# Layernorm finish and upsampling blend moved to VectorE, and a denser timetable, in a fused multi-scale attention kernel

## The chip, the core and the metric

The kernel runs on one core of a Trainium2 chip. TensorE (PE) multiplies, VectorE (DVE), ScalarE (ACT) and GpSimd (POOL) work on vectors, SyncE (SP) issues the DMAs. The metric is the time of one launch on the device in microseconds, the median of several runs.

## The reference

Eight sequences of 1024 tokens with 256 features go through a four-level attention, a residual layernorm, a feed-forward network and another residual layernorm. The part that the change touches is this:

```python
outs = []
for lvl in range(4):                        # strides 1, 2, 4, 8
    x = query[:, ::2**lvl, :]               # 1024, 512, 256, 128 tokens
    outs.append(_mha(x, in_w[lvl], in_b[lvl], out_w[lvl], out_b[lvl]))   # 16 heads of 16
current = outs[-1]
for lvl in (2, 1, 0):
    current = _upsample_linear(current, outs[lvl].shape[1])   # 0.75 near + 0.25 far
    current = current @ up_w[lvl].T + up_b[lvl]
    current = current + outs[lvl]
x = _layernorm(query + current)             # (x - mean) / sqrt(var + 1e-5), no gain
# then the gated feed-forward network and a second layernorm
```

## The kernel before, in words

The attention part lasts to about 2850 us of the span, the feed-forward part from there to the end; the change lies in the attention part alone. It works on one batch element after the other. The attention of one element is cut into 85 steps: a unit is a group of four heads and (at level 0) one half of 1024 query tokens, and a step is one block of 128 keys of a unit. In each step PE computes four 96x512 blocks of scores for the row maxima (L1015), four of the scores themselves (L1000), and eight value products (L1032); ACT takes two exponentials of 128x1024 (L760); DVE takes the four maxima over 512 columns (L839). The maxima's PSUM tile `p_m` has two halves: PE writes one while DVE reads the other.

Everything else is spread over the steps as side work. The projections (`proj`), value tiles (`v`), negated maxima (`neg`), output matmuls per level (`mid`), upsampled parts (`lift`, `row`) and the last output (`out`) each take one PSUM tile `p_a` in a step of its own. After each unit DVE transposes and normalizes its result (`turn`, `invert`, `spread`), POOL multiplies it (`attn`, L657).

The loop over the batch elements is software-pipelined: a prefix, a loop of seven bodies, and an end. A body runs from step 26.9 of one element to step 26.9 of the next, so the output part of an element runs at steps 10 to 24 of the next. Inside a body the order of the instructions is written by `timeline()`: it gives each task a time in steps, `places()` moves side jobs to free steps, and each engine sorts its tasks by that time plus an offset out of the table `LATER`. Each engine then does its tasks strictly in this order, waiting on semaphores for what the others have to deliver.

The output part of an element, in four jobs of 256 tokens, passes through these tasks: `fetch` (SP, six DMAs: the input tokens and the upsampled rows in two parts, L594 to L598), `sum` (POOL, two additions, L700 and L703, into a ring `s_ring` of four slots of 128 tokens; in the trace it is part of `a_c_f`), `out` (PE matmul, then DVE's addition, L879, which waits for `xt_summed`), and per half `stats` (DVE bn_stats L882, later POOL's power for rstd, L706, and the shift, L710), `gather` (DVE bn_aggr and the variance plus eps, L888 and L890), `finish` (ACT's scale and shift in place, L803, then SP's store to x1, L602). The sum of job n+2 waits for the stores of job n, as it writes over the same ring slots (`y_stored`). The half jobs are numbered 0 to 7.

`blend` builds the upsampled tokens of levels 3 and 2: ACT writes a part scaled by 0.75 and one scaled by 0.25 with scaled biases, and POOL adds shifted pieces of them (four additions for level 3, six for level 2). `scale` (two ACT operations of 128x1024, L808 and L810) and `keep` (SP) write the level 1 rows to memory, scaled by 0.75 and 0.25, from where `fetch` reads them.

## Time and profile before

| | us |
|---|---|
| median of three runs (4295.5 to 4300.24) | 4297.32 |
| the profiled execution | 4300.24 |
| its span | 4298.4 |
| PE busy | 3855.2 (90%) |
| DVE busy | 2566.8 (60%) |
| ACT busy | 2483.7 (58%) |
| POOL busy | 1211.1 (28%) |
| mean granted TensorE clock | 0.955 |

The profiled execution is one launch. Its span goes from its first to its last instruction, and what lies around it makes up the rest of its time. Times in the trace count from the span's start. Engines work beside each other, so the busy times do not add up. In a timeline row the bracket says how long the engine was idle ahead of the instruction and what released it; x2 is two instructions of the same kind in a row, and their time is given together.

### The profile page before, as it was taken

Reading aid. Unit: us, or ns where it says so; the run is one execution under the profiler, and the core shown is the slowest. Engines: PE = TensorE matmul, PEld = TensorE weight load, DVE = VectorE, ACT = ScalarE, POOL = GpSimd, SP = SyncE. Lnnn points to the kernel's source line nnn. Section 1 sums busy time; section 2 is a strip of 40 time slices with the busy share of each in tenths; the row PEclk is TensorE's granted clock in tenths of the full one; section 3 lists DMA queues with packets and bytes.
Section 4 is the critical chain, followed back from the end, with each engine's and each line's share of the span. In section 5 each row is a group of like instructions: output and inputs, shape, how many; then the busy total and the mean of one; then the engine's idle time right before and its main releaser. Section 6 shows DMA issues by size and latency. Waiting matters only on the chain. (4 is left out here: it accounts for less than half of the span.)

```text
span 4298.4 us, 69980 instructions
## 1 busy us (share of the span) xinstructions
PE 3855.2 (90%) x20881; PEld 2139.9 (50%) x20881; DVE 2566.8 (60%) x4681; ACT 2483.7 (58%) x3261; POOL 1211.1 (28%) x1144
## 2 busy tenths in 40 slices
PE   4589999989989999999999999918999999999998
PEld 2233334334333433333333333206887877877887
DVE  2377787787787787787787788643333333333333
ACT  1367767767767767767767766724444443444443
POOL 4234434435435434434434442210000000000000
PEclk6699999999999999999999999958999999999999
DMA  5344343344334344344344343151000000000000
GB/s 172 105 82 104 94 93 91 101 89 95 106 74 108 97 85 97 103 87 92 108 91 87 108 88 62 38 200 43 11 21 11 11 11 21 11 11 11 14 17 11
DMA packets 308845, 307.48 MB, mean 72 GB/s; under 512 B 75169, under 2 KB 285281, under 8 KB 308193
## 3 DMA queue, kind: packets, MB, share of 16 engines
q1 hardware_dynamic: 299200, 293.59, 27.7%
q10 hardware_dynamic: 9216, 8.39, 0.6%
q8 instruction: 243, 3.98, 0.4%
q14 instruction: 186, 1.52, 0.1%
HBM read 202.28 MB, written 96.47 MB: 70 GB/s over the span
## 5 line engine op out<-in xcount | busy, mean ns | idle before, releaser
L760 ACT ACTIVATE a_probs<-a_p_s 128x1024 f32<-128x1024 f32 x1360 | 1322.4, 1020 | 610.4 <-PE a_p_s L1000 603.2
L839 DVE TENSOR_REDUCE a_part_max<-a_p_m 128x1 f32<-128x512 f32 x2048 | 1338.5, 680 | 434.6 <-PE a_p_m L1015 429.7
L1015 PE MATMUL a_p_m<-a_k_st,a_q_st 96*128 96x512 bf16 (+2 forms) x2944 | 1010.3, 375 | 184.5 <-DVE a_part_max L839 85.4
L1395 PE MATMUL p_h<-f_h_hi,f_w_hi 128*128 128x512 f32 x2048 | 809.9, 395 | 40.0 <-issue 35.2
L1000 PE MATMUL a_p_s<-a_q_st,a_k_st 98*128 98x512 bf16 (+2 forms) x2944 | 822.2, 367 | 11.0 <-DMA a_q_st<-a_neg_bf 6.8
L1395 PE MATMUL p_h<-f_h_lo,f_w_hi 128*128 128x512 f32 x2048 | 806.3, 394 | 1.6 <-issue 1.6
L1015 PEld LDWEIGHTS a_p_m<-a_k_st,a_q_st 96*128 96x128 bf16 x2944 | 258.7, 97 | 1085.2 <-DVE a_part_max L839 692.0
L1032 PE MATMUL a_p_o<-a_probs,a_v_aug 128*17 128x512 f32 (+2 forms) x5888 | 729.3, 575 | 0.8 <-ACT a_probs L760 0.8
L1364 DVE TENSOR_TENSOR f_h_lo<-f_h_f,f_h_hi 128x512 fp32r<-128x512 f32 x256 | 177.1, 692 | 720.3 <-ACT f_h_hi L1277 720.3
L839 DVE TENSOR_REDUCE a_row_max<-a_p_m 128x1 f32<-128x512 f32 (+2 forms) x672 | 439.9, 680 | 176.3 <-PE a_p_m L1015 171.6
L1275 ACT ACTIVATE f_h_f<-p_h,f_sc 128x512 f32<-128x512 f32 x256 | 176.6, 690 | 583.2 <-PE p_h L1395 583.1
L1395 PEld LDWEIGHTS p_h<-f_h_hi,f_w_hi 128*128 128x128 f32 x2048 | 390.0, 190 | 110.5 <-issue 29.3
L1395 PEld LDWEIGHTS p_h<-f_h_lo,f_w_hi 128*128 128x128 f32 x2048 | 390.2, 191 | 97.3 <-issue 16.6
L1216 POOL TENSOR_TENSOR f_rstd<-f_var_eps,f_minus_half 128x1 f32<-128x1 f32 x64 | 35.1, 549 | 1410.3 <-DVE f_var_eps L1355 1410.3
L1000 PEld LDWEIGHTS a_p_s<-a_q_st,a_k_st 98*128 98x128 bf16 x2944 | 282.6, 99 | 264.6 <-ACT a_probs L760 25.5
L653 POOL TENSOR_TENSOR a_neg_bf<-a_neg_f,a_neg_bf 4x512 bf16<-4x512 f32 x120 | 138.0, 1150 | 365.7 <-ACT a_neg_bf L755 365.1
L643 POOL TENSOR_TENSOR a_qk<-a_qk,a_qk_bf 128x512 f32<-128x512 f32 x120 | 139.1, 1159 | 332.9 <-ACT a_qk_bf L748 332.9
L1032 PEld LDWEIGHTS a_p_o<-a_probs,a_v_aug 128*17 128x17 f32 x5888 | 103.2, 96 | 221.9 <-ACT a_probs L760 132.5
L908 PE MATMUL a_p_a<-a_x_hi,a_w_hi 128*128 128x512 f32 (+2 forms) x320 | 139.7, 437 | 78.2 <-POOL a_w_lo L632 61.2
L1395 PE MATMUL p_h<-f_xt_hi,f_w_hi 128*128 128x512 f32 x512 | 200.9, 392 | 1.4 <-DVE f_xt_lo L1316 1.4
L1395 PE MATMUL p_h<-f_xt_lo,f_w_hi 128*128 128x512 f32 x512 | 200.6, 392 | 0.0
L657 POOL TENSOR_TENSOR a_attn<-a_raw,a_attn 128x512 f32<-128x512 f32 x120 | 152.8, 1273 | 146.6 <-DVE a_attn L868 146.6
(116 smaller groups left out, 4552.5 us busy)
## 6 DMA issues: line engine op xcount, KB each, us to landing
qk_scratch<-a_qk_bf SPq DMA_DIRECT2D x96, 384.0 KB, 2.8
a_w_lo<-wqkv_inner SPq DMA_DIRECT2D x32, 768.0 KB, 4.3
a_q_st<-qk_scratch SPq DMA_DIRECT2D x192, 128.0 KB, 6.1
a_k_st<-qk_scratch SPq DMA_DIRECT2D x192, 128.0 KB, 6.5
a_q_st<-qk_scratch SPq DMA_DIRECT2D x336, 64.0 KB, 2.6
a_k_st<-qk_scratch SPq DMA_DIRECT2D x336, 64.0 KB, 2.7
a_a_lo<-a_attn SPq DMA_DIRECT2D x384, 32.0 KB, 1.9
a_o_lo<-wo_inner SPq DMA_DIRECT2D x24, 512.0 KB, 3.5
```

Of the source, the lines that this page charges most:

```text
L643: pool.tensor_tensor(out=rest, in0=rest, in1=bf[:, 0, :], op=ALU.subtract)\
L653: pool.tensor_tensor(out=neg_bf[:, n % 2, 1, :], in0=neg_f[:, :], in1=neg_bf[:, n % 2, 0, :], op=ALU.subtract).then_inc(neg_b.sem, 1)
L657: pool.tensor_tensor(out=attn[:, n % RING, :], in0=raw[:, n % 2, :], in1=attn[:, n % RING, :], op=ALU.mult)\
L760: act.activation(probs[:, s % 2, 2 * p:2 * p + 2, :], p_s[:, 2 * p:2 * p + 2, :], ACT.Exp, scale=HD ** -0.5).then_inc(exp_done.sem, 1)
L839: dve.reduce_max(out, src, AX.X).then_inc(max_read.sem, 1)
L908: ins = pe.matmul(out, a, c, start=n == 0, stop=n == len(terms) - 1)
L1000: ins = pe.matmul(p_s[:, j, i * size:(i + 1) * size], k_st[0:ROWS + 2, unit.halves[half], j, key:key + 128], q_st[0:ROWS + 2, unit.place, ...
L1015: ins = pe.matmul(p_m[:, n % 2, r * size:(r + 1) * size], q_st[0:ROWS, unit.place, j, q * 128:(q + 1) * 128], k_st[0:ROWS, unit.halves[kb] ...
L1032: ins = pe.matmul(p_o[32 * j:32 * j + HD + 1, at], v_aug[:, V_TILE[lvl] + kt, unit.head + j * parts + i, :], probs[:, n % 2, j, at], start ...
L1275: act.activation(h_f[:, v % 2, :], p_h[:, v % 4, :], ACT.Gelu, scale=sc[:, 8 + v:9 + v]).then_inc(deep_read.sem, 1)
L1364: dve.tensor_tensor(out=h_lo[:, (half + v // 8) % 2, v % 8, :], in0=h_f[:, v % 2, :], in1=h_hi[:, (half + v // 8) % 2, v % 8, :], op=ALU.s ...
L1395: ins = pe.matmul(out, a, c, start=first and n == 0, stop=last and n == len(terms) - 1)
```

## The change

The timetable changes in these places: the offset of POOL's `attn` (0.8) goes; the output jobs want places 3 steps apart, not 4 (they land at steps 10, 13, 16 and 19, before at 10, 14, 18 and 22, and two value jobs, `v`, go from 15 and 19 to 14 and 18); `row` 0 and 1 go from steps 66 and 67 to 64 and 66, `proj` 7 from 68 to 67, and `scale` and `keep` one step earlier. `finish` comes 1.8 steps behind its output job rather than 2.9. `fetch` 1 is later (step 90.65, not 83.3), `fetch` 3 and the sums are earlier. The tasks of `blend` follow each other at .15 steps, not .8.

Three tasks change engine or form. `blend` goes from POOL to DVE: ACT writes the upsampled part once, with the plain bias; DVE scales a copy by 0.75 and adds shifted pieces with a multiplication by 0.25 in the same instruction (scalar_tensor_tensor). `finish` goes from ACT to DVE, as a tensor_scalar that subtracts the mean and multiplies by rstd; so POOL's shift goes, and so does DVE's wait for a finished half ahead of `gather`. The last maximum of a level 0 unit, a reduction of 128x32 to 128x16, is a tensor_tensor with the operation max of the two columns.

```diff
@@ -214,7 +214,7 @@
 LATER = {
     "act": {"proj": .3, "neg": .2, "mid": .3, "lift": .3, "acut": .5},
     "dve": {"v": .3, "row": .3, "out": .3},
-    "pool": {"proj": .9, "neg": .6, "mid": .9, "ccut": .5, "acut": .8, "attn": .8, "xcut": .4, "wcut": .4, "ocut": .4, "stats": 1},
+    "pool": {"proj": .9, "neg": .6, "mid": .9, "ccut": .5, "acut": .8, "xcut": .4, "wcut": .4, "ocut": .4, "stats": 1},
...
@@ -240,14 +240,14 @@
     out_at = STEPS + 10
-    side.update(places([(("out", n), out_at + 4 * n) for n in range(4)], taken))
+    side.update(places([(("out", n), out_at + 3 * n) for n in range(4)], taken))
...
-            side.update(places([(("row", n), mid_at[lvl] + 6 + 2 * n) for n in range(2)], taken))
+            side.update(places([(("row", n), mid_at[lvl] + 5 + 2 * n) for n in range(2)], taken))
...
@@ -289,15 +289,15 @@
-            p += [(side[("lift", i)] + 1.5 + .8 * n, "blend", n + RUNS_DONE[lvl] - len(RUNS[lvl])) for n in range(len(RUNS[lvl]))]
+            p += [(side[("lift", i)] + 1 + .15 * n, "blend", n + RUNS_DONE[lvl] - len(RUNS[lvl])) for n in range(len(RUNS[lvl]))]
...
         at = side[("out", n)]
-        sum_at = 83 if n == 0 else at - 2.1
-        p.append((78 if n == 0 else (83 if n == 1 else side[("out", n - 1)] - 2.1) + .3, "fetch", n))
+        p.append((78 if n == 0 else max(sum_at, side[("out", n - 1)] - 6) + .8, "fetch", n))
+        sum_at = 83 if n == 0 else at - 1.5
         p.append((sum_at, "sum", n))
         for half in range(2):
-            p += [(at + .4 + .7 * half, "stats", 2 * n + half), (at + .75 + .7 * half, "gather", 2 * n + half), (at + 2.9 + .5 * half, "finish", 2 * n + half)]
+            p += [(at + .4 + .7 * half, "stats", 2 * n + half), (at + .75 + .7 * half, "gather", 2 * n + half), (at + 1.8 + .5 * half, "finish", 2 * n + half)]
...
-                        elif kind == "blend":
-                            lvl = 3 if n < RUNS_DONE[3] else 2
-                            run = n - (0 if lvl == 3 else RUNS_DONE[3])
-                            if run == 0:
-                                lift_read.wait(pool, it, 1 if lvl == 3 else 2)
...
-                            pool.tensor_tensor(out=fine[lvl - 1][:, :, dst:dst + size], in0=d_f[:, :, src:src + size],
-                                               in1=d_part[:, :, here:here + size], op=ALU.add).then_inc(fine_done.sem, 1)
...
-                            pool.wait_ge(rstd_done.sem, rstd_done.value(it, n + 1))
-                            pool.sem_inc(held.sem, 1)
-                            pool.tensor_scalar(shift[:, n % 2:n % 2 + 1], moments[:, n % 2, 0:1], rstd[:, n % 2:n % 2 + 1], -1.0, ALU.mult, ALU.mult)\
-                                .then_inc(shift_done.sem, 1)
...
-                                act.activation(d_part[:, m, 0:S], p_a[:, m * S:(m + 1) * S], ACT.Identity, bias=col_near[:, lvl - 1, m:m + 1], scale=0.75)
-                                ins = act.activation(d_f[:, m, 0:S], p_a[:, m * S:(m + 1) * S], ACT.Identity, bias=col_far[:, lvl - 1, m:m + 1], scale=0.25)
+                                ins = act.activation(d_f[:, m, 0:S], p_a[:, m * S:(m + 1) * S], ACT.Identity, bias=col[:, lvl - 1, CUP + m:CUP + m + 1])
                             ins.then_inc(lift_read.sem, 1)
-                        elif kind == "finish":
-                            act.wait_ge(shift_done.sem, shift_done.value(it, n + 1))
-                            act.activation(s_ring[:, n % 4, :], s_ring[:, n % 4, :], ACT.Identity, bias=shift[:, n % 2:n % 2 + 1],
-                                           scale=rstd[:, n % 2:n % 2 + 1]).then_inc(y_done.sem, 1)
...
-                                dve.reduce_max(slot, part_max[:, u % RING, :, :], AX.X).then_inc(max_done.sem, 1)
+                                dve.tensor_tensor(out=slot, in0=part_max[:, u % RING, :, 0], in1=part_max[:, u % RING, :, 1], op=ALU.max)\
+                                   .then_inc(max_done.sem, 1)
...
-                            y_done.wait(dve, it, n - 1)
-                            dve.sem_inc(held.sem, 1)
...
+                        elif kind == "finish":
+
+                            dve.wait_ge(rstd_done.sem, rstd_done.value(it, n + 1))
+                            dve.tensor_scalar(s_ring[:, n % 4, :], s_ring[:, n % 4, :], moments[:, n % 2, 0:1],
+                                              rstd[:, n % 2:n % 2 + 1], ALU.subtract, ALU.mult).then_inc(y_done.sem, 1)
+                        elif kind == "blend":
+                            lvl = 3 if n < RUNS_DONE[3] else 2
+                            run = n - (0 if lvl == 3 else RUNS_DONE[3])
+                            S = tokens(lvl)
+                            if run == 0:
+                                lift_read.wait(dve, it, 1 if lvl == 3 else 2)
+                                dve.tensor_scalar(d_part[:, :, 0:S], d_f[:, :, 0:S], 0.75, None, ALU.mult).then_inc(part_done.sem, 1)
+
+                                if lvl == 3:
+                                    xt_summed.wait(dve, earlier(it), 4)
+                                else:
+                                    kept.wait(dve, earlier(it), 1)
+                                part_done.wait(dve, it, 1 if lvl == 3 else 2)
+                            src, dst, size, here = RUNS[lvl][run]
+                            dve.scalar_tensor_tensor(out=fine[lvl - 1][:, :, dst:dst + size], in0=d_f[:, :, src:src + size],
+                                                     scalar=0.25, in1=d_part[:, :, here:here + size],
+                                                     op0=ALU.mult, op1=ALU.add).then_inc(fine_done.sem, 1)
```

What the order is around finish 3 on DVE (step 16). The value job is L849 before and L821 after, the maxima L839 and L810. Before:

```order
L849 TENSOR_TENSOR a_v_aug<-a_p_a,a_row 128x16x16 [waits a_value_mm]
L849 TENSOR_TENSOR a_v_aug<-a_p_a,a_row 128x16x16
L186 REGISTER_ALU
L888 BN_AGGR a_moments<-a_stats 128x2 [waits a_y_done,a_stats_done]
L890 TENSOR_SCALAR a_var_eps<-a_moments 128x1 [waits a_moments_done]
L829 REGISTER_ALU
L839 TENSOR_REDUCE a_part_max<-a_p_m 128x1 [waits a_max_mm]
L829 REGISTER_ALU
L839 TENSOR_REDUCE a_part_max<-a_p_m 128x1 [waits a_max_mm]
L842 TENSOR_REDUCE a_row_max<-a_part_max 128x16 [waits a_max_read]
```

After, where L865 is the finish (the first is finish 2, the second finish 3):

```order
L860 TENSOR_SCALAR a_var_eps<-a_moments 128x1 [waits a_moments_done]
L800 REGISTER_ALU
L810 TENSOR_REDUCE a_part_max<-a_p_m 128x1 [waits a_max_mm]
L800 REGISTER_ALU
L810 TENSOR_REDUCE a_part_max<-a_p_m 128x1 [waits a_max_mm]
L865 TENSOR_SCALAR a_c_f<-a_c_f,a_moments,a_rstd 128x256 [waits a_rstd_done]
L800 REGISTER_ALU
L810 TENSOR_REDUCE a_part_max<-a_p_m 128x1 [waits a_max_mm]
L800 REGISTER_ALU
L810 TENSOR_REDUCE a_part_max<-a_p_m 128x1 [waits a_max_mm]
L865 TENSOR_SCALAR a_c_f<-a_c_f,a_moments,a_rstd 128x256 [waits a_rstd_done]
L800 REGISTER_ALU
```

Two finishes that wait for rstd stand among the maxima; before, there is none on this engine.

POOL, from the attention product ahead of sum 2. L706 is rstd, L710 shift, L700 and L703 are the sum. Before:

```order
L657 TENSOR_TENSOR a_attn<-a_raw,a_attn 128x512 [waits a_spread_done]
L705 REGISTER_ALU
L706 TENSOR_TENSOR a_rstd<-a_var_eps,a_minus_half 128x1 [waits a_eps_done]
L710 TENSOR_SCALAR a_shift<-a_moments,a_rstd 128x1 [waits a_rstd_done]
L696 REGISTER_ALU
L186 REGISTER_ALU [waits a_fetched]
L700 TENSOR_TENSOR a_c_f<-a_d_room 128x512 [waits a_y_stored0,a_y_stored1]
L703 TENSOR_TENSOR a_c_f<-a_c_f,a_fine_room 128x512 [waits a_half_sum]
L705 REGISTER_ALU
L706 TENSOR_TENSOR a_rstd<-a_var_eps,a_minus_half 128x1 [waits a_eps_done]
L710 TENSOR_SCALAR a_shift<-a_moments,a_rstd 128x1 [waits a_rstd_done]
```

After, with L690 as rstd and L684 and L687 as the sum; the first L690 is rstd 2, the one behind sum 2 is rstd 3, then rstd 4:

```order
L655 TENSOR_TENSOR a_attn<-a_raw,a_attn 128x512 [waits a_spread_done]
L689 REGISTER_ALU
L690 TENSOR_TENSOR a_rstd<-a_var_eps,a_minus_half 128x1 [waits a_eps_done]
L680 REGISTER_ALU
L186 REGISTER_ALU [waits a_fetched]
L684 TENSOR_TENSOR a_c_f<-a_d_room 128x512 [waits a_y_stored0,a_y_stored1]
L687 TENSOR_TENSOR a_c_f<-a_c_f,a_fine_room 128x512 [waits a_half_sum]
L689 REGISTER_ALU
L690 TENSOR_TENSOR a_rstd<-a_var_eps,a_minus_half 128x1 [waits a_eps_done]
L689 REGISTER_ALU
L690 TENSOR_TENSOR a_rstd<-a_var_eps,a_minus_half 128x1 [waits a_eps_done]
```

Rstd 3 stands behind sum 2 in both orders. Further down, after only, sum 3 and rstd 5:

```order
L684 TENSOR_TENSOR a_c_f<-a_d_room 128x512 [waits a_y_stored3,a_fetched,a_y_stored2]
L687 TENSOR_TENSOR a_c_f<-a_c_f,a_fine_room 128x512 [waits a_half_sum]
L651 TENSOR_TENSOR a_neg_bf<-a_neg_f,a_neg_bf 4x512 [waits a_neg_hi]
L654 REGISTER_ALU
L655 TENSOR_TENSOR a_attn<-a_raw,a_attn 128x512 [waits a_spread_done]
L689 REGISTER_ALU
L690 TENSOR_TENSOR a_rstd<-a_var_eps,a_minus_half 128x1 [waits a_eps_done]
```

Rstd 5 stands behind sum 3, a negated maximum (L651) and an attention product (L655).

SP, around the loads of stack 8 (twelve DMAs, of which the first and last rows stand). L602 is the store of a finished half. Before:

```order
L598 DMA a_fine_room<-up_far 64x256 x4
L186 REGISTER_ALU [waits a_stored0,a_stored1]
L542 DMA a_q_st<-qk_scratch 16x8x512 [waits a_score_mm]
L542 DMA a_k_st<-qk_scratch 16x8x512
...
L542 DMA a_q_st<-qk_scratch 16x8x512
L542 DMA a_k_st<-qk_scratch 16x8x512
L600 REGISTER_ALU
L602 DMA x<-a_c_f 128x256 [waits a_y_done]
L600 REGISTER_ALU
L602 ISA [waits a_y_done]
L602 DMA x<-a_c_f 128x256
```

After, where L600 is the store and L540 the loads:

```order
L596 DMA a_fine_room<-up_far 64x256 x4
L598 REGISTER_ALU
L600 DMA x<-a_c_f 128x256 [waits a_y_done]
L186 REGISTER_ALU [waits a_stored0,a_stored1]
L540 DMA a_q_st<-qk_scratch 16x8x512 [waits a_score_mm]
L540 DMA a_k_st<-qk_scratch 16x8x512
...
L540 DMA a_q_st<-qk_scratch 16x8x512
L540 DMA a_k_st<-qk_scratch 16x8x512
L598 REGISTER_ALU
L600 ISA [waits a_y_done]
L600 DMA x<-a_c_f 128x256
```

One of the two stores now stands ahead of the twelve loads, the other behind them as before.

## Rows read from the trace of the kernel before

**Rows 1.** The page, part 1: busy time, share and instructions of each engine.

```profile
PE 3855.2 (90%) x20881; PEld 2139.9 (50%) x20881; DVE 2566.8 (60%) x4681; ACT 2483.7 (58%) x3261; POOL 1211.1 (28%) x1144
```

**Rows 2.** Busy times in windows: start:end, length, busy of each, PEclk, DMA share, GB/s.

```profile
1675.00:2000.00 325.00, 304.56 (x1844) 126.73 (x1842) 250.45 (x462) 230.26 (x292) 141.45 (x132) 0.98 0.42 97
```

**Rows 3.** Timeline of ScalarE, 1728 to 1735: start us, duration, line, operation, [idle before <-releaser].

```profile
1728.01 1.94 ACT L760 ACTIVATE a_probs<-a_p_s 128x1024 f32<-128x1024 f32 x2 [0.60 <-PE a_p_s L1000]
...
1731.42 1.94 ACT L760 ACTIVATE a_probs<-a_p_s 128x1024 f32<-128x1024 f32 x2
...
1734.55 1.94 ACT L760 ACTIVATE a_probs<-a_p_s 128x1024 f32<-128x1024 f32 x2 [1.19 <-PE a_p_s L1000]
```

**Rows 4.** Timeline of ScalarE, 1773 to 1797.

```profile
1773.07 1.94 ACT L760 ACTIVATE a_probs<-a_p_s 128x1024 f32<-128x1024 f32 x2 [2.31 <-PE a_p_s L1000]
...
1777.32 1.94 ACT L760 ACTIVATE a_probs<-a_p_s 128x1024 f32<-128x1024 f32 x2 [2.31 <-PE a_p_s L1000]
...
1779.15 1.06 ACT L808 ACTIVATE a_d_room<-a_c_f 128x1024 f32<-128x1024 f32 x1
...
1785.83 0.69 ACT L743 ACTIVATE a_qk<-a_p_a,a_col 128x512 f32<-128x512 f32 x1 [1.53 <-POOL a_qk_bf L649]
...
1797.14 1.94 ACT L760 ACTIVATE a_probs<-a_p_s 128x1024 f32<-128x1024 f32 x2
```

**Rows 5.** Timeline of ScalarE, 1909 to 1944.

```profile
1909.50 1.94 ACT L760 ACTIVATE a_probs<-a_p_s 128x1024 f32<-128x1024 f32 x2
...
1915.50 0.60 ACT L803 ACTIVATE a_c_f<-a_c_f,a_shift,a_rstd 128x256 f32<-128x256 f32 x1 [2.45 <-POOL a_shift L710]
...
1922.33 1.94 ACT L760 ACTIVATE a_probs<-a_p_s 128x1024 f32<-128x1024 f32 x2 [2.06 <-PE a_p_s L1000]
...
1944.02 1.94 ACT L760 ACTIVATE a_probs<-a_p_s 128x1024 f32<-128x1024 f32 x2 [1.19 <-PE a_p_s L1000]
```

**Rows 6.** Busy times in two windows around the slow matmuls of step 23.

```profile
1932.00:1937.00 5.00, 3.17 (x16) 0.82 (x16) 4.93 (x14) 2.71 (x3) 1.80 (x2) 1.00 0.08 20
1937.00:1941.00 4.00, 3.92 (x14) 0.89 (x15) 2.81 (x8) 0.12 (x1) 2.34 (x5) 0.57 0.44 143
```

**Rows 7.** Timeline of SP's queue, 1896 to 1920: DMA issues.

```profile
1896.36 0.64 SPq L542 DMA_DIRECT2D a_q_st<-qk_scratch  x1
...
1904.35 1.07 SPq L602 DMA_DIRECT2D x<-a_c_f  x2
...
1919.58 0.38 SPq L602 DMA_DIRECT2D x<-a_c_f  x1
```

**Rows 8.** The stores of L602, issued 1900 to 1930: from issue to landing.

```profile
DMA to landing us min/median/max: 1.7/5.7/6.9
```

**Rows 9.** Timeline of POOL, 1911 to 1926.

```profile
1911.75 1.26 POOL L700 TENSOR_TENSOR a_c_f<-a_d_room 128x512 f32<-128x512 f32 x1 [7.87 <-DMA x<-a_c_f]
...
1914.44 0.55 POOL L706 TENSOR_TENSOR a_rstd<-a_var_eps,a_minus_half 128x1 f32<-128x1 f32 x1
...
1915.42 1.15 POOL L653 TENSOR_TENSOR a_neg_bf<-a_neg_f,a_neg_bf 4x512 bf16<-4x512 f32 x1
...
1919.77 1.27 POOL L657 TENSOR_TENSOR a_attn<-a_raw,a_attn 128x512 f32<-128x512 f32 x1
...
1926.12 1.26 POOL L700 TENSOR_TENSOR a_c_f<-a_d_room 128x512 f32<-128x512 f32 x1 [4.09 <-DMA x<-a_c_f]
```

**Rows 10.** Waits of POOL, 700 to 2650: total us, times, longest.

```profile
POOL a_c_f L700 <- DMA x<-a_c_f: 72.0, 12, 8.5
```

**Rows 11.** Timeline of VectorE, step 16.

```profile
1905.99 1.29 DVE L839 TENSOR_REDUCE a_part_max<-a_p_m 128x1 f32<-128x512 f32 x2
```

**Rows 12.** VectorE's groups by line, shapes apart: busy us, mean ns of one, idle.

```profile
L1332 DVE SCALAR_TENSOR_TENSOR f_h_f<-p_h,f_sc,f_gate 128x512 f32<-128x512 f32 x128 | 96.1, 751 | 159.6 <-PE p_h L1395 139.8 <-ACT f_gate L1249 19.8
...
L1341 DVE TENSOR_SCALAR f_s_ring<-f_s_ring,f_moments,f_rstd 128x256 f32<-128x256 f32 x64 | 26.1, 408 | 2.7 <-POOL f_rstd L1216 2.7
...
L842 DVE TENSOR_REDUCE a_row_max<-a_part_max 128x16 f32<-128x32 f32 x64 | 11.9, 186 | 2.2
```

More of the change, by code:

```diff
@@ L375, in attention @@
         stats, moments = sb("stats", [128, 2, 6]), sb("moments", [128, 2, 2])
-        var_eps, rstd, shift, minus_half = sb("var_eps", [128, 2]), sb("rstd", [128, 2]), sb("shift", [128, 2]), sb("minus_half", [128, 1])
-        col_near, col_far = sb("col_near", [128, LEVELS, 2]), sb("col_far", [128, LEVELS, 2])
+        var_eps, rstd, minus_half = sb("var_eps", [128, 2]), sb("rstd", [128, 2]), sb("minus_half", [128, 1])
         d_f, d_part = d_room[:, 0:512].rearrange("p (c t) -> p c t", c=2), d_room[:, 512:1024].rearrange("p (c t) -> p c t", c=2)
@@ L422, in attention @@
         out_mm, out_read = sig("out_mm", 4, lead=4), sig("out_read", 4, lead=4)
[L423 to L424 removed]
+        stats_done, moments_done, eps_done, rstd_done, y_done = (sig(name, 8) for name in ("stats_done", "moments_done", "eps_done", "rstd_done", "y_done"))
         y_stored = [sig(f"y_stored{i}", 2, 16, lead=2) for i in range(4)]
@@ L717, in _ @@
                 act.wait_ge(const_in.sem, 48)
-                act.activation(col_near[:, :, :], col[:, :, CUP:CCOLS], ACT.Copy, scale=0.75).then_inc(up_done.sem, 1)
-                act.activation(col_far[:, :, :], col[:, :, CUP:CCOLS], ACT.Copy, scale=0.25).then_inc(up_done.sem, 1)
-                act.wait_ge(up_done.sem, 2)
-                y_done.open(act)
                 def steps(tasks, iteration, prev):
```

11 lines of the change are left out of this document (1 added, 10 removed).

## The prediction

> **What bounds the kernel now.** I read the page first: TensorE is busy for 90% of the span [rows 1]. Then the busy times of a stretch of one loop body, from 1675 to 2000 us: PE 304.56 of 325 us, DVE 250.45, ACT 230.26, POOL 141.45, granted clock 0.98 [rows 2]. So the body is PE's, and about 20 us of it are pauses, and slow matmuls behind them. The feed-forward half (2850 to 4298 us) is not touched. What a pause costs is read from the pace of the exponentials, two per step, in ScalarE's timeline: a step with a head group's transposes takes 3.41 us (1728.01 to 1731.42), one with nothing beside it 3.13 (to 1734.55) [rows 3], one with a side job of twelve matmuls 4.25 (1773.07 to 1777.32) [rows 4]. There are 85 steps to a body, and seven bodies.
>
> Three crowded places of a body are longer than that pace allows. Steps 17 to 19 take from 1909.50 to 1922.33, 12.8 us, where a lighter step (3.3) and two side jobs want 11.8; steps 20 to 24 take to 1944.02, 21.7 us, where two side-free steps (6.3), two with transposes (6.8) and one side job (4.2) want 17.3 [rows 5]. Steps 68 to 71 take 19.8 us (1777.32 to 1797.14), where three side jobs and one step with transposes want 16.2 [rows 4]. In the second place the clock is part of the price: with DVE busy 4.93 of 5.00 us, PE has 3.17 of them, and in the four us behind, PE runs at 0.57 of full speed (its lower level, 1.2 GHz), 3.92 us busy [rows 6]. At full speed that work is 2.2 us: a pause of this size costs 1.7 us behind itself.
>
> **What waits around the output part.** Here the queues matter. On SP the twelve loads of stack 8 are issued from 1896.36, and only then the two stores of finished rows (1904.35); the next store goes out at 1919.58 [rows 7]. Over this stretch a store takes 1.7 us at best, 5.7 in the middle and 6.9 at worst from issue to landing [rows 8]; the 6.9 is that of the store behind the loads, and it lands at 1911.3. POOL's sum 2 overwrites the ring slot that this store reads. It starts at 1911.75 after 7.87 us of waiting, its two halves take 2.7 us to the rstd behind it, which takes 0.55 from 1914.44; sum 3 then starts at 1926.12 after 4.09 us [rows 9]. This is so in all bodies: POOL waits for these stores 12 times between 700 and 2650 us, 72.0 us in all [rows 10]. Today POOL can afford it. What the wait reaches is ScalarE: its finish at 1915.50 has waited 2.45 us for the shift of that rstd [rows 5], and VectorE takes out 2 a little late.
>
> **The change, part by part.** The stalls come first.
>
> *Finish on VectorE, one wait too early: +8.6 and +1.7 us per body.* The finish was at 2.9 steps behind its output job on ScalarE; now it is at 1.8 on VectorE, and the jobs are 3 steps apart. Finish 3 so falls to step 16.15, and by the orders it stands in front of the maxima of step 16 on DVE, waiting for rstd 3. POOL has rstd 3 still behind sum 2, and sum 2 still waits for store 1, which on SP still stands behind the twelve loads; store 0 alone goes in front of them. Nothing in this chain became earlier: the loads wait for the same scores, so store 1 is issued near 1904.5, lands near 1911.2, sum 2 starts at once and takes 2.6 to 2.7 us, and rstd 3 ends about 1914.4 (1914.99 before). VectorE reaches finish 3 at about 1905.3 (in its place two maxima start at 1905.99 [rows 11], and the value pair ahead of them has moved a step up). It stands still for 9.1 us, and behind it in its queue are the maxima on whose reading PE's next matmuls depend. PE has two buffers of maxima, so it goes on for about 0.5 us: 8.6 us of pause. Behind a pause the clock is low: 1.7 us more, as above. ScalarE's wait of 2.45 us goes in return, and is counted with the gains.
>
> *The second stall: +3.0 and +1.7.* By the order, rstd 5 stands on POOL behind sum 3, a negated maximum and an attention product. Sum 3 waits for stores 2 and 3, which SP sends behind fetch 3 at about 1919.6, and starts near 1925.2 (1926.12 before). Then 2.7, 1.15, 1.27 and 0.55 us [rows 9] give 1930.9. VectorE leaves the first stall at 1914.8 and has three steps to finish 5, 10.9 us and the 1.7 of the low clock: 1927.4. It waits 3.5 us, of which 0.5 is covered.
>
> *Spacing and side jobs: −4.1.* Out 3 leaves the crowd of steps 20 to 24, which is 4.4 too long; 17 to 19 are 1.0 too long, since ScalarE waits there. Of these 5.4 us I take 4.1, for finish 6 and 7 now stand among the transposes of that place (0.41 us each [rows 12]), and others stand at steps 12 and 13. Where the side job goes it costs what it cost, so it is no gain by itself.
>
> *Row, scale, keep and proj 7 one step earlier: −2.5.* ScalarE does two scale operations of 1.06 us there, then waits 1.53 us for POOL before the read of the eighth projection (1785.83) [rows 4], and the raw copy that VectorE and then PE wait for is behind it. One step of distance may take away all of the 3.6 us or little: I take 2.5.
>
> *The loop's seam: −0.8.* The attention product no longer has its offset of 0.8 steps on POOL, and around step 26, where a body ends, the last stores go out ahead of what SP loads. No row prices that; I bound it by 0 and by the 1.7 us of one clock dip [rows 6], and take half.
>
> *Blends on VectorE: +1.5.* Per body there are two scalings and ten mixed additions. VectorE's tensor_scalar of 128x256 takes 408 ns [rows 12], and a maximum over 512 columns 645 within a pair [rows 11], so 0.17 us and 0.93 ns per column: 1.1 us for the two scalings, 3.1 us for ten additions of 1536 columns in all (from above, the mixed addition of 128x512 out of PSUM at 751 ns [rows 12] adds a sixth). Of these 4.2 us, up to 1.5 lies beside each of two side steps, where four maxima fill only 2.7 of 4.25 us; 1.2 is left at least, and I take 1.5. Were none hidden, it would be 4.2. POOL's additions, two of ScalarE's four activations and the shifts fall away, but nothing waits for these engines there: 0.
>
> *The last maximum as one tensor_tensor of two columns: −0.2.* It took 186 ns [rows 12], eight times per body. At best half of that goes, and only where DVE is full, in two or three of the eight; at worst nothing.
>
> Sum per body: 8.6 + 1.7 + 3.0 + 1.7 − 4.1 − 2.5 − 0.8 + 1.5 − 0.2 = +8.9 us, times seven +62. The last batch's output part, where nothing lies beside, gets about 1.5 us shorter (four pairs of shifts, 0.4 us with the gap each, of which PE's end sees most). The profiled execution took 4300.2 us (span 4298.4), so 4361 on its scale; the median of the runs is 2.9 lower: 4358 us.
>
> **A rule for the store.** Of loads queued ahead of a store, the row says: 6.9 us against 1.7 [rows 8]. The Trainium skill ("DMA: Bandwidth & Descriptors", section "Queues, rings and completion order") says that each DMA engine starts its descriptors in ring order, but that completion is not first in, first out per issuing engine. By its second half the store could land long before the loads; the trace sides with the first half, as it landed behind them. What the other reading would make is the second rival.
>
> **The rivals.**
>
> *A, faster: the stalls do not reach PE.* Were rstd 3 and rstd 5 ready when VectorE comes to them, or were PE and the maxima far enough ahead, only the rest would count: −4.1 − 2.5 − 0.8 + 1.5 − 0.2 = −6.1 per body, −43 in all, 4253 us. It decides where both stalls together cost less than 6.1 us a body. For it speaks that POOL loses its late offset and its shifts. Against it: sum 2's start lies on the store's landing in every body, and 9.1 us are three steps, more than two buffers hold. Chance 0.10.
>
> *B, a milder loss: store 1 lands early.* If it lands in the 1.7 us of an undisturbed store [rows 8], sum 2 is done at 1908.7 and rstd 3 at 1909.3: the first stall is 5.5 us shorter, the body +3.4, the kernel +24, 4319 us. For it: store 0 no longer goes with it, so the queue is shorter by one. Against: the loads in front are the same. Chance 0.17.
>
> *C, no change.* If besides B the second stall goes too, since the first one's delay gives POOL time, the body stands at −1.3, 4287 us by the same sum, and with one clock dip of 1.7 us kept per body at +0.4: 4299. Chance 0.05.
>
> *D, heavier.* If all of the 4.2 us of blends shows, and the moved jobs gain nothing at 68 to 71 (+2.5), the body is at +14.1: 4395 us. Chance 0.13.
>
> **How the numbers follow.** The forecast, 4358 us, has 0.55; its own range is 4335 to 4378. The range for 8 in 10 goes from B's lower side to D: 4310 to 4392; below are A and C with 0.15, above it 0.05. A measurement of this kernel can tell 0.2% (8.6 us) from no change: faster 0.10, same 0.05, slower 0.85.
>
> **What would show it.** In the profile after: VectorE's finish idle on POOL's rstd for some 9 and 3 us per body, in two of its eight; POOL's sum 2 still waiting for the store, its starts within 0.4 us of a landing; steps 16 or 17 some 9 us longer, two dips of the clock there; steps 20 to 24 near 17.5 us and 68 to 71 near 17.3. DVE's busy time rises by about 7 us per body, ACT's and POOL's fall by about 5 and 4. If store 1 is found to land within 2 us, it is B; if the finishes have no idle time ahead of them, it is A and my reading of the order is wrong. The mean growth of a body tells the cases apart: +9 us for the forecast, +3 for B, −6 for A.

## The result and the profile after

The changed kernel is slower, by nearly three times what was forecast: median 4472.86 us of 4 runs (4460.4 to 4476.26) against 4298.78 us for the kernel before, ratio 1.0399, 95% interval 1.0377 to 1.0422. That is +174 us where +60 was forecast, and it lies outside the stated range. The sign was right, and so were place and size of the stalls of steps 13 to 25 (+12.7 us a body for +10.9); most of what was missed lies in three other places, which the forecast took as gains or as mostly hidden.

The kernel before was measured again beside each experiment below (medians from 4293.2 to 4301.0 us), and each ratio is taken against the runs beside it. Two executions at a granted clock of 0.55 to 0.56, one of the kernel before (6429.32 us) and one of the timetable alone (6429.66 us), are left out of the ratios.

The page's busy line, to be read beside [rows 1]:

```profile
PE 3904.1 (87%) x20881; PEld 2152.1 (48%) x20881; DVE 2665.8 (60%) x4841; ACT 2448.1 (55%) x3163; POOL 1160.8 (26%) x1000
```

DVE has 99 us more than before, ACT 36 and POOL 50 less, but the time goes into pauses of PE and into slow matmuls behind them: PE's busy time rose by 49 us for the same 20881 matmuls. ScalarE's timeline, as in [rows 5], one body later:

```profile
2007.34 1.94 ACT L736 ACTIVATE a_probs<-a_p_s 128x1024 f32<-128x1024 f32 x2 [2.08 <-PE a_p_s L992]
...
2020.94 1.94 ACT L736 ACTIVATE a_probs<-a_p_s 128x1024 f32<-128x1024 f32 x2 [0.76 <-PE a_p_s L992]
...
2028.58 1.94 ACT L736 ACTIVATE a_probs<-a_p_s 128x1024 f32<-128x1024 f32 x2 [1.80 <-PE a_p_s L992]
2039.60 1.94 ACT L736 ACTIVATE a_probs<-a_p_s 128x1024 f32<-128x1024 f32 x2 [9.08 <-PE a_p_s L992]
```

Step 16 takes 13.6 us (2007.34 to 2020.94) and step 19 takes 11.0 (2028.58 to 2039.60). VectorE's timeline shows what stands there:

```profile
2015.40 0.41 DVE L865 TENSOR_SCALAR a_c_f<-a_c_f,a_moments,a_rstd 128x256 f32<-128x256 f32 x1 [8.85 <-POOL a_rstd L690]
...
2031.75 1.35 DVE L865 TENSOR_SCALAR a_c_f<-a_c_f,a_moments,a_rstd 128x256 f32<-128x256 f32 x1 [3.91 <-POOL a_rstd L690]
```

These are finish 3 and finish 5, and their waits are 8.85 and 3.91 us, where the forecast had 9.1 and 3.5. POOL's and SP's timelines give the chain behind the first:

```profile
2004.68 0.37 SPq L600 DMA_DIRECT2D x<-a_c_f  x1
```

```profile
2012.16 1.26 POOL L684 TENSOR_TENSOR a_c_f<-a_d_room 128x512 f32<-128x512 f32 x1 [8.93 <-issue]
...
2014.82 0.55 POOL L690 TENSOR_TENSOR a_rstd<-a_var_eps,a_minus_half 128x1 f32<-128x1 f32 x1
```

The longest landing of a store issued from 1990 to 2012 is 7.3 us, so the one of 2004.68 lands by 2012.0, and sum 2 starts at 2012.16. The profile puts this wait down to "issue"; that it was the store is read from the landing time beside it. The granted clock falls behind the pause, from 0.92 to 0.50, in windows as in [rows 6]:

```profile
2008.00:2015.00 7.00, 1.29 (x11) 1.08 (x10) 0.00 (x0) 1.28 (x2) 2.66 (x3) 0.92 0.53 73
2015.00:2019.00 4.00, 2.52 (x10) 0.36 (x10) 3.55 (x7) 0.00 (x0) 0.37 (x1) 0.50 0.53 164
```

To see where the rest is, I took the start of every step's first exponential from the trace and compared the mean length of each step over six bodies. Sums over stretches of steps, against before, in us per body:

| steps | changed | attn offset | maximum | blends | timetable | finish | all four undone |
|---|---|---|---|---|---|---|---|
| 13 to 25 | +12.7 | −0.2 | −0.4 | −0.3 | +7.6 | −1.0 | −2.0 |
| 35 to 46 | +0.8 | 0 | +0.4 | +0.4 | 0 | 0 | +0.3 |
| 47 to 51 | +3.2 | +3.2 | 0 | 0 | 0 | 0 | 0 |
| 52 to 55 | +4.6 | 0 | 0 | +4.8 | 0 | 0 | +0.4 |
| 56 to 63 | +2.7 | 0 | +3.9 | 0 | 0 | 0 | −0.3 |
| 64 to 72 | −2.1 | −0.3 | +0.1 | −0.6 | −2.8 | −0.5 | −2.8 |
| 79 to 84 | +2.7 | +2.7 | 0 | 0 | 0 | 0 | 0 |
| body | +25.0 | +5.5 | +3.7 | +3.6 | +5.2 | −1.8 | −3.5 |

Stretches left out differ by 0.9 us or less. Seven times 25.0 is 175 us, near the whole difference of 174 (the mean leaves out the first body and the end). The other columns are experiments, told next.

### The profile page after: what moved, and what is told of

Same layout as the page of the kernel before. It is cut to its first block and busy times, and to the rows that moved or that the text cites. A ratio compares the mean times of both kernels' runs of the same rounds, so it can differ in the third digit from the quotient of the medians.

```text
span 4467.1 us, 69697 instructions
## 1 busy us (share of the span) xinstructions
PE 3904.1 (87%) x20881; PEld 2152.1 (48%) x20881; DVE 2665.8 (60%) x4841; ACT 2448.1 (55%) x3163; POOL 1160.8 (26%) x1000
## 5 line engine op out<-in xcount | busy, mean ns | idle before, releaser
L810 DVE TENSOR_REDUCE a_part_max<-a_p_m 128x1 f32<-128x512 f32 x2048 | 1337.9, 680 | 436.7 <-PE a_p_m L1007 431.9
L1007 PE MATMUL a_p_m<-a_k_st,a_q_st 96*128 96x512 bf16 (+2 forms) x2944 | 1024.5, 380 | 252.2 <-DVE a_part_max L810 153.7
L1024 PE MATMUL a_p_o<-a_probs,a_v_aug 128*17 128x512 f32 (+2 forms) x5888 | 740.6, 583 | 0.8 <-ACT a_probs L736 0.8
L810 DVE TENSOR_REDUCE a_row_max<-a_p_m 128x1 f32<-128x512 f32 (+2 forms) x672 | 440.3, 680 | 187.3 <-PE a_p_m L1007 182.1
L655 POOL TENSOR_TENSOR a_attn<-a_raw,a_attn 128x512 f32<-128x512 f32 x120 | 152.9, 1274 | 548.8 <-DVE a_attn L840 548.8
L651 POOL TENSOR_TENSOR a_neg_bf<-a_neg_f,a_neg_bf 4x512 bf16<-4x512 f32 x120 | 137.9, 1149 | 344.2 <-ACT a_neg_bf L731 343.5
```

Source lines behind the costliest of these rows:

```text
L651: pool.tensor_tensor(out=neg_bf[:, n % 2, 1, :], in0=neg_f[:, :], in1=neg_bf[:, n % 2, 0, :], op=ALU.subtract).then_inc(neg_b.sem, 1)
L655: pool.tensor_tensor(out=attn[:, n % RING, :], in0=raw[:, n % 2, :], in1=attn[:, n % RING, :], op=ALU.mult)\
L810: dve.reduce_max(out, src, AX.X).then_inc(max_read.sem, 1)
L1007: ins = pe.matmul(p_m[:, n % 2, r * size:(r + 1) * size], q_st[0:ROWS, unit.place, j, q * 128:(q + 1) * 128], k_st[0:ROWS, unit.halves[kb] ...
L1024: ins = pe.matmul(p_o[32 * j:32 * j + HD + 1, at], v_aug[:, V_TILE[lvl] + kt, unit.head + j * parts + i, :], probs[:, n % 2, j, at], start ...
```

## Experiments: one part at a time on the kernel before

**POOL's attention offset alone.**

```diff
-"acut": .8, "attn": .8, "xcut": .4
+"acut": .8, "xcut": .4
```

> The kernel before with one edit: POOL's attention product loses its late offset of 0.8 steps. Theory 1 (the loss of 174 us has three causes: the waits on rstd, this order on POOL, and VectorE operations that share something with POOL): in the trace of the changed kernel POOL stands idle 5.58 us ahead of an attention product with the split of a projection behind it, and step 47 grows from 4.24 to 7.36 us and step 79 from 4.24 to 7.35. So here +6.5 us a body, +45 us, about 4343 us, ratio 1.010. Rival (all of the loss comes from the waits on rstd and what they shift): 0, 4297 us.

4333.32 us, ratio 1.0088 (1.0070 to 1.0107). Theory 1 holds: the loss is in steps 47 to 51 and 79 to 84, as in the changed kernel, 5.5 us a body for 6.5 expected. In the changed kernel, POOL's timeline reads at step 47:

```profile
2146.89 1.27 POOL L655 TENSOR_TENSOR a_attn<-a_raw,a_attn 128x512 f32<-128x512 f32 x1 [5.58 <-DVE a_attn L840]
2148.12 1.16 POOL L641 TENSOR_TENSOR a_qk<-a_qk,a_qk_bf 128x512 f32<-128x512 f32 x1
```

and ScalarE's:

```profile
2151.38 0.69 ACT L719 ACTIVATE a_qk<-a_p_a,a_col 128x512 f32<-128x512 f32 x1 [3.57 <-POOL a_qk_bf L647]
```

POOL waits 5.58 us for VectorE's transposes, and behind it in its queue is the split of a projection that was ready at 2144.5, when ScalarE had written it. The next projection's read waits for that split, and PE waits 1.99 us for this read before it can use the PSUM tile again. In the run with this edit alone PE has this wait 6 times between 700 and 2650 us, 11.9 us in all; in the kernel before its list has no such row. The offset had kept the product behind the split.

**The last maximum alone.**

```diff
-dve.reduce_max(slot, part_max[:, u % RING, :, :], AX.X)
+dve.tensor_tensor(out=slot, in0=part_max[..., 0], in1=part_max[..., 1], op=ALU.max)
```

> The kernel before with one edit: the last maximum of a level 0 unit is a tensor_tensor of two SBUF columns instead of a reduction. Theory 1: the operation takes 0.17 us alone and up to 2.58 us beside a POOL operation, as in the trace of the changed kernel (mean 0.77 us), so the groups beside POOL's long subtraction of 3.44 us push step 56 from 3.13 to 5.04 us; +2 to +4 us a body, +14 to +28 us, about 4315 us. Rival: the long ones are an effect of the changed timetable; 0 to -0.2 us a body, 4296 us, with a mean of 0.17 us.

4323.54 us, ratio 1.0065 (1.0048 to 1.0081). The operation that was to save some of 186 ns [rows 12] took 751 ns in the mean; its line in the trace (shortest, median and longest in ns), and the worst one beside POOL's row, in this run:

```profile
L842 DVE TENSOR_TENSOR a_row_max<-a_part_max x64: 174/376/3061, 260.9 to 2793.1; 128x16 f32<-128x16 f32 x64
```

```profile
1745.37 3.06 DVE L842 TENSOR_TENSOR a_row_max<-a_part_max 128x16 f32<-128x16 f32 x1
```

```profile
1744.96 3.44 POOL L632 TENSOR_TENSOR a_w_lo<-a_w_lo,a_w_hi 128x1536 fp32r<-128x1536 f32 x1
```

POOL's operation ends at 1748.40 and VectorE's at 1748.43. Of all 64, 43 started while a POOL operation ran. Of these, 42 ended 0.03 to 0.05 us after it; the last came 0.05 us before POOL's end and took 0.18 us, and the 21 others took 0.17 to 0.18 us. So in this trace the operation, with its two inputs from SBUF, waits until POOL's running operation is over. The reduction before took 185 to 188 ns in all 64 cases, beside POOL or not. The Trainium skill says this ("SBUF — State Buffer", section "SBUF: two separate sides"): a VectorE operation with two SBUF inputs and a GpSimd operation that reads SBUF contend for a shared port pair, an exclusive lock held for the whole instruction. The trace agrees, at up to 3.06 us for an operation of 128x16; the forecast had not used it.

**POOL's split moved away from that maximum**, on top of the edit above.

```diff
-"wcut": .4
+"wcut": 1.4
```

> The kernel before with the last maximum as a two-input operation, and POOL's splits of the weights (3.44 us each) one step later. In the run with the maximum alone, this operation took 0.18 us with POOL idle and 3.06 us in step 56, where POOL's 3.44 us split begins ahead of it. Theory (it stands still until POOL's operation ends): the one of step 56 takes under 1.5 us now, step 56 and 57 lose most of their 3.9 us, about 4300 us. Rival (the operation is slow for its own data at that place): as before, 3.1 us and 4323 us.

4328.68 us, ratio 1.0065 (1.0047 to 1.0083). A miss of mine: in POOL's order the split still follows the same product with nothing between, so it started 0.41 us ahead of the maximum as before, and that took up to 3.06 us again. The run repeats the finding; whether moving the split away helps is not shown.

**Blends on VectorE, close together and spread.**

```diff
-side[("lift", i)] + 1.5 + .8 * n, "blend"   (on POOL)
+side[("lift", i)] + 1 + .15 * n, "blend"    (on DVE, close)
+side[("lift", i)] + 1 + .8 * n, "blend"     (on DVE, spread)
```

> The kernel before with one edit: the blends on VectorE, close behind each other, and the upsampled part written once. Theory 1: step 52 goes from 3.13 to 7.3 us as in the changed kernel, steps 35 to 40 lose 0.6; +5 us a body, +35 us, 4332 us, and the two-input operations beside POOL take longer than their size says. Rival (the recorded estimate, hidden but for 1.5 us a body): +10 us, 4308 us.

> The kernel before with the blends on VectorE, 0.8 steps apart as before instead of 0.15. Close together they cost 4.8 us in step 52 and 53 and nearly nothing elsewhere, for some 4.5 us of VectorE time. Theory (five of them in a row ahead of maxima starve PE once, and the low clock follows): spread, one per step, at most 1.5 us a body, about 4303 us. Rival (the instruction is slow beside POOL's work, whatever its place): +3 us a body or more, over 4315 us.

Close together 4327.43 us, ratio 1.0075 (1.0055 to 1.0095); spread 4296.96 us, ratio 1.0005 (0.9991 to 1.0020). VectorE's timeline in the first, and PE's:

```profile
2060.93 2.57 DVE L892 SCALAR_TENSOR_TENSOR a_fine_room<-a_d_room 128x256 f32<-128x256 f32 x3
```

```profile
2064.16 0.61 PE L1018 MATMUL a_p_m<-a_k_st,a_q_st 96*128 96x512 bf16 x1 [2.71 <-DVE a_part_max L824]
```

Three additions in a row, of 256, 254 and 2 columns, hold the maxima back by 2.6 us; PE pauses, and from 2064 to 2067 its granted clock is 0.50. The same work spread costs nothing that can be measured, so the move to VectorE is not dear by itself. But the block is not the whole price either, for the additions also have two inputs from SBUF. The largest, close together and then spread:

```profile
L892 DVE SCALAR_TENSOR_TENSOR a_fine_room<-a_d_room 128x256 f32<-128x256 f32 x16 | 11.6, 725 | 0.0
```

```profile
L892 DVE SCALAR_TENSOR_TENSOR a_fine_room<-a_d_room 128x256 f32<-128x256 f32 x16 | 6.6, 415 | 0.0
```

Close together, 29 of all 80 additions started while a POOL operation ran, and they took up to 1.12 us; spread, 15 did, and the longest took 0.44. The three in a row above took 2.6 us, where their lengths without POOL (0.42, 0.41 and 0.15) add up to 1.0: 1.6 us of the hold is waiting for POOL. Spreading took away both the block and the meeting with POOL, and no run parts the two.

**The timetable alone**, with the finish on ScalarE at 2.9 steps and the blends on POOL.

```diff
-out_at + 4 * n ... mid_at[lvl] + 6 + 2 * n ... sum at - 2.1
+out_at + 3 * n ... mid_at[lvl] + 5 + 2 * n ... sum at - 1.5
```

> The kernel before with the timetable of the output part and the rows alone (output jobs 3 steps apart, row, scale, keep one step earlier, fetch and sum moved); the finish stays on ScalarE at 2.9 steps, blends stay on POOL. Both theories: steps 68 to 71 gain 2 us a body (37.9 to 35.8 for steps 64 to 72 in the changed kernel). Theory 1: the waits on rstd reach only ScalarE, steps 13 to 24 lose 0 to 3 us against before; between -2 and +1 us a body, 4283 to 4304 us. Rival (the spacing itself is what costs, whatever engine the finish is on): +8 us a body or more, over 4350 us.

4339.46 us, the median of three executions, ratio 1.0108 (1.0086 to 1.0129). The truth lay between the two named outcomes, nearer the rival: steps 64 to 72 gain 2.8 us, and steps 13 to 25 lose 7.6, with no finish on VectorE at all. Step 16 takes 10.7 us and step 19 takes 7.1. VectorE's output addition, which needs the same sum, waits for POOL 12 times between 700 and 2650 us, 29.5 us in all (in the kernel before, the list of VectorE's waits in that stretch has no row for it).

**The finish alone**, at 2.9 steps.

```diff
-act.activation(s_ring[..], bias=shift, scale=rstd)            # and POOL's shift
+dve.tensor_scalar(s_ring[..], moments, rstd, subtract, mult)
```

> The kernel before with the finish on VectorE at its old place of 2.9 steps behind the output job, and POOL's shift gone; timetable, blends and all else as before. The recorded estimate put the stall on this move: if VectorE's wait on rstd is the cause, +8 us a body or more, over 4350 us. Theory now: with four steps between output jobs, rstd 3 is ready (step 17.9) before VectorE comes to finish 3 (step 18.25), and ScalarE's wait of 2.45 us goes; the eight tensor_scalars of 0.41 us cost a little where VectorE is full: -2 to +1.5 us a body, 4280 to 4305 us.

4289.98 us, ratio 0.9986 (0.9975 to 0.9996). The move itself costs nothing and gains a little. Its waits on rstd are 1.2 us in all between 700 and 2650 us, against 60.3 in the changed kernel.

## Experiments: which wait fills steps 13 to 25

**Rstd ahead of the sum**, in the changed kernel.

```diff
-"ocut": .4, "stats": 1
+"ocut": .4, "stats": .3
```

> The changed kernel with one edit: POOL's offset of the rstd tasks is 0.3 steps instead of 1, so that rstd 3 and rstd 5 stand before sum 2 and sum 3; stores, loads and the output additions stay where they are. If VectorE's wait on rstd is the step that costs (the recorded forecast), steps 13 to 25 lose nearly all of their excess of 12.7 us: +1 to +3 left, about 4400 us. If the output addition, which waits for the same sum, would stop VectorE in any case (theory now): about the 7.6 us of the timetable alone are left, -5 us a body, about 4438 us.

4428.01 us, ratio 1.0300 (1.0280 to 1.0319): −45 us against the changed kernel. Of the 12.7 us of steps 13 to 25, 6.6 are left, near the timetable's 7.6, and the stall has moved to the output addition, one step on. VectorE's timeline:

```profile
1991.40 0.69 DVE L851 TENSOR_TENSOR a_c_f<-a_p_a,a_c_f 128x512 f32<-128x512 f32 x1 [6.35 <-POOL a_c_f L687]
```

So two waits on the same sum stand one behind the other, and the forecast named the first. Taking it away gave half of the loss in steps 13 to 25.

**The finish early at the old spacing**: the kernel before with the finish on VectorE and the rows one step earlier, and

```diff
-(at + 2.9 + .5 * half, "finish"
+(at + 1.8 + .5 * half, "finish"
```

> The finish on VectorE and the rows one step earlier, as in the fastest kernel so far (4274.5 us), and the finish at 1.8 steps instead of 2.9, output jobs 4 steps apart. With it steps 13 to 25 were 2.5 us under before in one kernel and 1.1 us under without; but sum 2 here stays at 16.75, ahead of rstd 3, so finish 3 at step 17.15 may wait for it as forecast. If the wait does not bite: -1 us a body, 4267 us. If it does: +2 us a body or more, 4290 us.

4318.75 us, ratio 1.0057 (1.0040 to 1.0073); the same without the early finish is 4274.5 (below). The wait of the forecast bites by itself, at the old spacing and with the sums where they were: steps 13 to 25 take 5.5 us more than before, where without the early finish they take 1.1 less. It comes six times in the stretch from 700 to 2650 us, 32.2 us in all; VectorE's timeline in this run:

```profile
1922.00 1.23 DVE L884 TENSOR_SCALAR a_c_f<-a_c_f,a_moments,a_rstd 128x256 f32<-128x256 f32 x1 [5.79 <-POOL a_rstd L706]
```

**The spacing undone** in the changed kernel (`3 * n` to `4 * n`).

> The changed kernel with the output jobs 4 steps apart again, everything else as changed (finish on VectorE at 1.8 steps). By the order POOL then takes rstd 3 before sum 2, and the output addition comes a step later. Theory 1 (the spacing of 3 steps is what makes steps 16 and 19 long: output addition and finish come before a sum that waits for a store): steps 13 to 25 go from 66.3 to about 53 us, -13 us a body, about 4382 us. Rival (a finish on VectorE at 1.8 steps is too early at any spacing): -4 us a body at most, over 4440 us.

4379.52 us, ratio 1.0188 (1.0165 to 1.0212): −93 us, as expected. Steps 13 to 25 are 2.5 us shorter than before, with the finish still at 1.8 steps on VectorE. The edit does two things: the output addition comes a step later, and, as the sums keep their new distance of 1.5 steps ahead of it, POOL takes rstd 3 before sum 2. VectorE's list of waits has neither the sum nor rstd in it.

**The loads out of the way**: stack 8 at step 18.4 in the changed kernel, in the timetable alone, and in the kernel before with the rows earlier.

```diff
-stack_at.update({8: 14, 9: 30, 10: 46})
+stack_at.update({8: 18.4, 9: 30, 10: 46})
```

> The changed kernel with one edit: the twelve loads of stack 8 at step 18.4 instead of 14, behind the stores that sum 2 and sum 3 wait for. Theory 1 (steps 16 and 19 are long because these stores land behind the loads): stores land in about 1.7 us, VectorE's finishes wait less than 1 us, steps 13 to 25 fall from 66.3 to about 52 us, -14 us a body, about 4375 us; the other causes (POOL's order, two-input operations) stay. Rival (the additions on POOL are late by themselves at 3 steps, or the loads now come too late for the maxima of step 25): less than -3 us a body, over 4450 us.

> The kernel before with the denser timetable and the loads of stack 8 at step 18.4; the finish on ScalarE, blends on POOL. Theory 1: the timetable alone gave 10.7 and 7.1 us for steps 16 and 19 and +46 us, and that is the stores behind the loads; without it steps 13 to 25 take about 51 us (61.5 with the timetable alone, 53.6 before) and the gain of the rows of 2.8 us a body is left: -5 us a body against before, about 4260 us. Rival (the spacing of three steps is too short for the chain of sum, output, statistics): over 4310 us.

> The kernel before with two edits: row 0 and 1 with what hangs on them one step earlier, and stack 8 at step 18.4; output jobs 4 steps apart. Theory: -2.8 us a body for steps 64 to 71 (seen with the timetable alone), and -0.9 to -2 for steps 17 to 23, since sum 2 no longer waits 7.9 us for the store: -4 to -5 us a body, about 4262 us. Rival (POOL's wait costs nothing at a spacing of 4 steps): -20 us, 4273 us.

4450.89 us, ratio 1.0360 (1.0343 to 1.0378); 4311.52 us, 1.0036 (1.0026 to 1.0047); 4320.92 us, 1.0052 (1.0035 to 1.0069). Step 16 went from 13.3 to 4.2 us in the first: its stall was the store behind the loads. But step 19 grew from 11.0 to 15.1. SP's timeline in the first, and from issue to landing of the two stores in it:

```profile
1996.62 3.04 SPq L596 DMA_DIRECT2D a_fine_room<-up_far  x4
1999.90 1.09 SPq L600 DMA_DIRECT2D x<-a_c_f  x2
2001.31 0.65 SPq L540 DMA_DIRECT2D a_q_st<-qk_scratch  x1
```

```profile
DMA to landing us min/median/max: 11.7/11.8/12.0
```

The stores of 1999.90 were issued ahead of the loads and landed at 2011.9 and later, while a load of 2001.31 had landed at 2004.9. POOL's sum 3 waits 9.0 us for them. In the timetable alone with the same move it is the same: the two stores of 1914.97 and 1915.67, with the loads right behind, took 12.2 and 12.0 us, and sum 3 waits for them; the two of 1899.13 and 1899.84, with nothing behind them for nearly 8 us, took 1.7. So the order of issue does not by itself protect a store. This is the rule that the forecast quoted and set aside (the Trainium skill, "DMA: Bandwidth & Descriptors", "Queues, rings and completion order": completion is not first in, first out); in that the trace now agrees with it. But loads behind a store do not always delay it. In the changed kernel the single store ahead of the loads, issued at 1995.89 with the first load 0.7 us behind it, has this time to its landing:

```profile
DMA to landing us min/median/max: 2.1/2.1/2.1
```

In all seven bodies it is 1.8 to 2.1 us, as the forecast took it, against 9.2 to 13.1 us for the two stores in the seven bodies of the moved loads. What makes the difference is open. In the third kernel a negated maximum issued behind the loads landed late, and PE waited for it, which is what this kernel loses in steps 13 to 25 (+6.2 us); PE's timeline:

```profile
1951.66 1.03 PE L1000 MATMUL a_p_s<-a_q_st,a_k_st 98*128 98x512 bf16 x2 [6.79 <-DMA a_q_st<-a_neg_bf]
```

All three expectations were too low for these late landings.

## Experiments: sums of parts

**Two parts undone in the changed kernel**: attention offset and reduction back.

> The changed kernel with POOL's offset for the attention product and the reduction for the last maximum restored. Theory 1 (the causes add up): singly they cost 38 and 28 us, steps 47, 79 to 81 and 56, 57 and 40 return to the values before; -66 us, about 4405 us. Rival (in the changed kernel they overlap with the other stalls): less than -35 us, over 4438 us.

4439.08 us, ratio 1.0334 (1.0309 to 1.0360): −34 us, half of the sum of the single prices. Steps 47 to 51, 56 to 63 and 79 to 84 return to before, but steps 13 to 25 go from +12.7 to +16.6. At step 16 the later product now stands on POOL between sum 2 and rstd 3, and finish 3 waits 11.08 us where it had waited 8.85. At step 19 it follows rstd 5, right behind another POOL operation, and finish 5 takes 2.57 us instead of 1.35; POOL's sum 3 also waits longer for its store there (7.06 us for 4.15). The parts do not simply add.

**All four undone**: spacing, offset, reduction, and blends spread.

```diff
-out_at + 3 * n
+out_at + 4 * n
-"acut": .8, "xcut"
+"acut": .8, "attn": .8, "xcut"
-dve.tensor_tensor(out=slot, ..., op=ALU.max)
+dve.reduce_max(slot, part_max[:, u % RING, :, :], AX.X)
-+ 1 + .15 * n, "blend"
++ 1 + .8 * n, "blend"
```

> The changed kernel with the four suspected places put back at once: output jobs 4 steps apart, POOL's offset of the attention product, the reduction for the last maximum, blends 0.8 steps apart; finish and blends stay on VectorE, rows stay one step earlier. If these four are the whole loss, the rest is what gained: steps 13 to 25 -2.5 us, 64 to 72 -2.8, against +0.8 and +1.8 us early in the body and at the seam: about -2.5 us a body, 4276 us. If something else costs too: over 4300 us.

4274.44 us, ratio 0.9961 (0.9948 to 0.9974). Undoing these four takes away the whole loss; what is left of the change gains 21 us by the medians.

**The gaining parts on the kernel before**: finish on VectorE at 2.9 steps, rows one step earlier (best1); and with stack 8 at step 12.05 (best2).

> The two parts of the change that gained by themselves, on the kernel before: the finish on VectorE at 2.9 steps, and the rows, scale, keep and projection 7 one step earlier. If they add up: -1.8 us a body (finish alone) and -2.8 (steps 64 to 71 in the run with the timetable alone): -4.6 us a body, -32 us, about 4263 us. Rival: the seam around step 26 takes up half of it, 4280 us.

> The same as best1, and stack 8 loaded from step 12.05 rather than 14, ahead of fetch 2, where no store and no negated maximum goes out. Moved to 18.4 the loads delayed stores issued ahead of them and a negated maximum behind them, each by 7 to 12 us. Theory: at 12.05 the stores of finish 0 and 1 land in 2 to 6 us, POOL's sum 2 starts 2 to 5 us earlier, but at a spacing of 4 steps nobody waits for it now: 0 to -1 us a body against best1, about 4260 us. Rival: fetch 2 behind the loads comes too late, output job 2 waits: +2 us a body against best1.

4274.54 us, ratio 0.9945 (0.9923 to 0.9967), and 4277.88 us, ratio 0.9955 (0.9936 to 0.9975). The first is 4.0 us a body shorter, for 4.6 expected; the second is no better. So best1 and all four undone beat both kernels, by about 0.5%, with intervals that overlap.

## Why the forecast was wrong, step by step

- *Finish, one wait too early (+8.6, +1.7) and the second stall (+3.0, +1.7).* The waits are there and of the size: 8.85 us for 9.1, 3.91 for 3.5. With the gain of the spacing (−4.1) the forecast had +10.9 us for steps 13 to 25; measured +12.7. The chain behind them, store, sum 2, rstd 3, is there too. What the step had wrong is that it gave this chain a single victim, the finish. In these steps the early finish by itself costs (+5.5 at the old spacing, −1.1 without it), and the timetable by itself costs as well (+7.6, with the finish on ScalarE), since the output addition waits for the same sum 2 and comes 3 steps on instead of 4. I had not asked what else waits for that sum. The engine of the finish is not the reason (finish alone −1.0). With both undone by one edit, the spacing of 4 steps with rstd 3 ahead of sum 2, it is −2.5.
- *Spacing and side jobs (−4.1).* The gain is there, beside the stalls: the crowd of steps 20 to 24 went (21.5 us before in the mean, 17.7 in the changed kernel). But by itself the timetable is no gain in steps 13 to 25: its price, 7.6 us net, stands at steps 16 and 19, and the forecast had put all of it on the finish.
- *Row, scale, keep and proj 7 (−2.5).* Right: −2.8 in the timetable alone, −2.1 in the changed kernel.
- *The seam with POOL's attention offset (−0.8).* Wrong sign: steps 26 to 34 +0.5 us, and the offset costs 5.9 us in steps 47 to 51 and 79 to 84. I priced it at the seam, since no row prices it there, and did not follow it to the projections, where POOL has the split of a projection right behind an attention product. This is the largest miss: 41 us in seven bodies.
- *Blends on VectorE (+1.5).* Measured +4.8 in steps 52 to 55 in their own run, and +0.4 when spread. The sum of the instructions was 4.2 us, estimated; spread they take 4.1, close together 5.7, and the 1.6 more is waiting for POOL, which the sum had at nothing. And "beside two side steps" failed: at .15 steps apart they stand in one block in front of the maxima. The bound "none hidden", 4.2, was nearer than the value taken.
- *The last maximum (−0.2).* Wrong sign: measured +3.7 alone. The price came from the size of the operands, and the wait for POOL's running operation, up to 3.06 us, was put at nothing.
- *What put the time outside the range.* The offset, the blends and the last maximum were booked at +0.5 us a body together and measured +12.8 (5.5, 3.6 and 3.7, each alone). This is most of the 16 us by which a body (+25.0 for +8.9) was missed.
- *The range.* Its upper end took in only the costs that I had found. Three parts without a direct row were booked at −5.1 us a body (−4.1, −0.8, −0.2), a fourth, the blends, as mostly hidden, and no case held that several of them fail together.

## What to carry to other kernels

When tasks are sorted by one table, a removed offset is a changed order at every place where the task occurs: walk the whole cycle, engine by engine, and name what stands behind each waiting instruction. When a wait is found, list everything that waits for the same thing before calling one of them the cause; undoing one gave half. Moving work to the engine that feeds the bottleneck was cheap in single pieces (finish alone 0.9986, blends spread 1.0005) and dear in a block that also met POOL's operations (blends close 1.0075). Before an operation with two SBUF inputs goes to VectorE, look at what POOL runs at that time.
